# Row-to-column turning of the expert tiles: PE transposes against block-wise ScalarE writes and VectorE 32x32 turns

## The reference

```python
x = x + autocorrelation(layernorm(x), ctx, ctx)      # 8 heads, top 12 lags, soft-weighted shifted sums
n = layernorm(x)                                      # (x - mean) / sqrt(var + 1e-5), 2048 features
q = n @ Wq.T                                          # 16 values per row
scores = q @ keys.T                                   # 64 experts
gate = softmax over the 16 best scores, 0 elsewhere
z = (n @ A.T) as 64 experts x 8, times gate           # 512 values per row
x = x + (z @ B.T) * 2.0
```

## Time and profile before

| what | us |
|---|---|
| median of 3 runs | 2157.5 (2156.28 to 2159.11) |
| the profiled execution, whole | 2156.57 |
| its span, first to last instruction | 2154.8 |
| one step of the expert tiles | 25.33 |

### The profile page before, as it was taken

The page is one execution under the profiler, slowest core; times in us unless marked ns, Lnnn a source line. Parts: engine busy times, 40 slices in busy tenths (PEclk is TensorE's granted clock), DMA queues, the critical chain, the costliest instruction groups (busy, mean ns, idle before and its releaser), DMA issues.

```text
span 2154.8 us, 29239 instructions
## 1 busy us (share of the span) xinstructions
PE 2115.7 (98%) x8920; PEld 1328.0 (62%) x8920; DVE 1673.8 (78%) x4051; ACT 1337.5 (62%) x3051; POOL 1561.3 (72%) x965
## 2 busy tenths in 40 slices
PE   5999999999999999999999999999999999999999
PEld 2455455455455455454454454888888888888887
DVE  7999999999999999999999999644444444444443
ACT  4786786786786786786765646644444455445441
POOL 6999999999999999999999988633343433333420
PEclk9999999999999999999999999999999999999999
DMA  7232333333333332333221246544545444444431
GB/s 282 97 108 103 120 111 103 120 111 103 121 109 103 121 109 103 122 109 103 103 89 64 83 168 239 171 158 166 175 164 174 159 166 165 158 166 172 164 119 59
DMA packets 110705, 287.50 MB, mean 133 GB/s; under 512 B 7168, under 2 KB 7296, under 8 KB 109568
## 3 DMA queue, kind: packets, MB, share of 16 engines
q1 hardware_dynamic: 110592, 286.19, 38.3%
HBM read 219.06 MB, written 67.11 MB: 133 GB/s over the span
## 4 chain that ended last, share of the span: by engine, by line
PE 82%; DVE 7%; POOL 6%; ACT 2%; issue 2%; DMA 1%; SPq 0%; DVEq 0%; ACTq 0%; POOLq 0%
PE pair L755 11%; PE pair L749 8%; PE out L581 6%; PE out L582 6%; PE out L583 6%; PE z L583 5%; PE z L582 5%; PE z L581 5%; PE pair L644 5%; PE evac L631 4%; PE evac L655 4%; PE evac L656 4%; PE lag L698 4%; PE pair L745 4%; PE tp L600 2%; POOL r_f L1804 2%
## 5 line engine op out<-in xcount | busy, mean ns | idle before, releaser
L1838 POOL TENSOR_TENSOR rows<-rows,cin 128x1024 f32<-128x1024 f32 x48 | 117.0, 2437 | 325.7 <-DMA rows<-out_dram 273.6
L755 PE MATMUL pair<-r_f,back 128*128 128x512 f32 x768 | 342.7, 597 | 0.5 <-DVE prod L1035 0.5
L1804 POOL TENSOR_TENSOR r_f<-prod 128x1024 f32<-128x1024 f32 x128 | 303.0, 2378 | 9.3 <-DVE prod L1033 7.4
L755 PEld LDWEIGHTS pair<-r_f,back 128*128 128x128 f32 x768 | 143.0, 190 | 192.7 <-issue 146.5
L749 PE MATMUL pair<-w_sb,wts 128*128 128x512 f32 x512 | 225.1, 592 | 1.4 <-ACT w_sb L1625 0.9
L1480 ACT ACTIVATE xn<-tp 128x512 f32<-128x512 f32 x94 | 55.1, 586 | 231.0 <-PE tp L600 230.9
L581 PE MATMUL z<-a_hi,xt 128*128 128x512 f32 x496 | 195.9, 395 | 0.0
L581 PE MATMUL out<-b_hi,zt_hi 128*128 128x512 f32 x492 | 194.3, 395 | 0.0
L583 PE MATMUL z<-a_hi,xt 128*128 128x512 f32 x496 | 193.4, 390 | 0.0
L582 PE MATMUL z<-a_lo,xt 128*128 128x512 f32 x496 | 193.3, 390 | 0.0
L582 PE MATMUL out<-b_lo,zt_hi 128*128 128x512 f32 x492 | 191.6, 389 | 0.0
(11 more groups left out here) (234 smaller groups left out, 5576.8 us busy)
## 6 DMA issues: line engine op xcount, KB each, us to landing
out_dram<-att_sb SPq DMA_DIRECT2D x32, 1024.0 KB, 4.2
rows<-out_dram SPq DMA_DIRECT2D x64, 512.0 KB, 3.8
cin<-out_dram SPq DMA_DIRECT2D x63, 512.0 KB, 4.0
xin<-in_x_dram SPq DMA_DIRECT2D x63, 512.0 KB, 4.1
vf<-in_ctx_dram SPq DMA_DIRECT2D x31, 1024.0 KB, 5.1
out_dram<-rows SPq DMA_DIRECT2D x62, 512.0 KB, 2.8
xf<-in_x_dram SPq DMA_DIRECT2D x30, 1024.0 KB, 5.3
stat_in<-in_x_dram SPq DMA_DIRECT2D x27, 1024.0 KB, 5.1
```

Source lines behind the costliest of these rows:

```text
L755: return nc.tensor.matmul(pair_ps[:, bank, :], back[:, 3 * bank + n, :], r_f[:, row, :], start=n == 0, stop=n == 2)
L1804: nc.gpsimd.tensor_tensor(dst, prod[:, slot, 0:2, :], prod[:, slot, 2:4, :], ALU.add).then_inc(add_done, 1)
L1838: nc.gpsimd.tensor_tensor(half, first, other, op).then_inc(c_added, 1)
```

## The change

For tiles 4 to 31 (`spread(t)`) PE's 16 transposes and ACT's four copies out of PSUM go. In their place ACT writes the normalized rows in 16 operations of 32 partitions x 512 (`norm_blocks`): rows of partition group c and features of group b go to partition group b, column block c. DVE then turns `xn` in place in four operations of 128x512, each made of 32x32 blocks (`turn_spread`). Together these make the full transpose, with the features in another order, which the host gives to A and Wq as well (`laid_out`), and `norm_rows` to tiles 0 to 3. The low part is now taken from `xt_full` in SBUF, not from PSUM. Of the 16 blocks, 12 are written at the end of the ACT step before, behind `tile_scale` and `copy_queries`, the last four behind `zt_high`. PE makes the queries of tile u+1 ahead of the last output bank of step u. DVE's order changes: the first half of the statistics goes ahead of the turns, the turns ahead of route, the second half and tile_mean ahead of gate_z, and invert_root ahead of add_out 2.

```diff
@@ -247,6 +247,7 @@
         x2_added, stat2_step, root2_done, norm2_ready = (
             sem("x2_added"), sem("stat2_step"), sem("root2_done"), sem("norm2_ready"))
         xn_ready, tp_ready = sem("xn_ready"), sem("tp_ready")
+        xn_part = sem("xn_part")
         tp_hi, tp_lo, tp_full = sem("tp_hi"), sem("tp_lo"), sem("tp_full")
         q_ready, q_copied, sc_ready, sc_copied = sem("q_ready"), sem("q_copied"), sem("sc_ready"), sem("sc_copied")
         route_step, gate_exp, gate_step, gate_ready = (
@@ -384,8 +385,19 @@
 
             return xt[:, low, 0:KN, :] if is_step(u, TT) else (zt_lo if low else zt_hi)[:]
 
+        FIRST_SPREAD = 4
+        SPREAD = P // 4
+        SPREAD_PARTS = 16
+
+        def spread(t):
+            return not (isinstance(t, int) and t < FIRST_SPREAD)
+
         def later_tile(u):
             return not (isinstance(u, int) and u + 2 >= TT)
+
+        def ahead(u):
+
+            return later_tile(u) and spread(u + 2)
 
         def each_tile(eng, body):
             body(0, -1, 3, True, False, True)
@@ -833,8 +845,9 @@
                     queries(0, 2)
                     queries(0, 3)
                 elif a and not is_step(u, 1):
-                    for q in range(4):
-                        queries(u, q)
+                    if is_step(u, 2):
+                        for q in range(4):
+                            queries(u, q)
                     pe.wait_ge(tp_lo, tp_at(u, 3) + 1)
                 def turn_z(t=u):
                     pe.wait_ge(zg_ready, t)
@@ -891,14 +904,17 @@
                                         b_hi[:, q, m, :], b_lo[:, q, m, :], m == 0, m == KN - 1)
                     last.then_inc(out_ready, 1)
 
-                if f and not is_step(u, 0):
+                if f and not (is_step(u, 0) or spread(u + 1)):
                     for q in range(4):
                         turn_tile(u + 1, q)
                 if b:
-                    if not f:
+                    if not f or spread(u + 1):
                         pe.wait_ge(zt_hi_done, u)
                         pe.wait_ge(zt_lo_done, u)
                     for q in range(4):
+                        if q == 3 and f and not is_step(u, 1):
+                            for part in range(4):
+                                queries(u + 1, part)
                         out_bank(q)
                         if is_step(u, TT - 1) and q == 1:
                             turn_z(TT)
@@ -992,8 +1008,16 @@
 
                 dve.wait_ge(tp_hi, tp_at(t, q) + 1)
                 part = slice(4 * q, 4 * q + 4)
-                nc.vector.tensor_tensor(xt[:, 1, part, :], tp_ps[bank_of(t, q)][:], xt[:, 0, part, :].bitcast(F32),
+                turned_x = xt_full[:, q, :, :] if spread(t) else tp_ps[bank_of(t, q)][:]
+                nc.vector.tensor_tensor(xt[:, 1, part, :], turned_x, xt[:, 0, part, :].bitcast(F32),
                                         ALU.subtract).then_inc(tp_lo, 1)
+
+            def turn_spread(t, q):
+
+                if q == 0:
+                    dve.wait_ge(xn_part, SPREAD_PARTS * (t - FIRST_SPREAD + 1))
+                part = xn[:, q * 512:(q + 1) * 512]
+                nc.vector.transpose(part, part).then_inc(tp_full, 1)
 
             def half_statistics(t, slot, h):
                 dve.wait_ge(x2_added, 2 * t + h + 1)
@@ -1359,30 +1383,33 @@
                     return
                 if not is_step(u, TT):
                     zt_low()
+                if later_tile(u):
+                    half_statistics(u + 2, (r + 3) % RING, 0)
+                if f and spread(u + 1):
+                    for q in range(4):
+                        turn_spread(u + 1, q)
                 if a:
                     route()
                 if f:
                     tile_low(u + 1, 0)
+                add_out(0)
+                if f:
                     tile_low(u + 1, 1)
-                add_out(0)
-                if a:
-                    gate_z()
-                if f:
-                    tile_low(u + 1, 2)
-                if later_tile(u):
-                    half_statistics(u + 2, (r + 3) % RING, 0)
-                add_out(1)
-                if f:
-                    tile_low(u + 1, 3)
                 if later_tile(u):
                     half_statistics(u + 2, (r + 3) % RING, 1)
                     tile_mean(u + 2)
+                if a:
+                    gate_z()
+                add_out(1)
+                if f:
+                    tile_low(u + 1, 2)
+                    tile_low(u + 1, 3)
                 if is_step(u, TT - 1):
                     zt_low(TT)
+                if later_tile(u):
+                    invert_root(u + 2)
                 add_out(2)
                 add_out(3)
-                if later_tile(u):
-                    invert_root(u + 2)
 
             each_tile(dve, tile_step)
 
@@ -1476,8 +1503,9 @@
 
             def tile_high(t, q):
                 n = tp_at(t, q)
-                act.wait_ge(tp_ready, n + 1)
-                nc.scalar.activation(xt_full[:, q, :, :], tp_ps[bank_of(t, q)][:], ACT.Copy).then_inc(tp_full, 1)
+                if not spread(t):
+                    act.wait_ge(tp_ready, n + 1)
+                    nc.scalar.activation(xt_full[:, q, :, :], tp_ps[bank_of(t, q)][:], ACT.Copy).then_inc(tp_full, 1)
                 act.wait_ge(tp_full, n + 1)
                 nc.scalar.activation(xt[:, 0, 4 * q:4 * q + 4, :], xt_full[:, q, :, :], ACT.Copy).then_inc(tp_hi, 1)
 
@@ -1506,8 +1534,22 @@
 
             def norm_rows(t, slot):
                 act.wait_ge(norm2_ready, 2 * t + 2)
-                nc.scalar.activation(xn[:], rows[slot][:], ACT.Identity, bias=shift2[:],
-                                     scale=rstd2[:]).then_inc(xn_ready, 1)
+                nc.scalar.activation(xn[:].rearrange("p (k b i) -> p b k i", b=4, k=KD),
+                                     rows[slot][:].rearrange("p (b k i) -> p b k i", b=4, k=KD),
+                                     ACT.Identity, bias=shift2[:], scale=rstd2[:]).then_inc(xn_ready, 1)
+
+            def norm_blocks(t, slot, blocks):
+
+                if blocks[0] == 0:
+                    act.wait_ge(norm2_ready, 2 * t + 2)
+                    act.wait_ge(tp_lo, tp_at(t - 1, 3) + 1)
+                by_block = xn[:].rearrange("p (k c i) -> p k c i", k=KD, c=4)
+                for c in blocks:
+                    own = slice(SPREAD * c, SPREAD * (c + 1))
+                    for b in range(4):
+                        nc.scalar.activation(by_block[SPREAD * b:SPREAD * (b + 1), :, c, :],
+                                             rows[slot][own, b * 512:(b + 1) * 512].rearrange("p (k i) -> p k i", k=KD),
+                                             ACT.Identity, bias=shift2[own], scale=rstd2[own]).then_inc(xn_part, 1)
 
             act.wait_ge(consts_set, 2)
             nc.scalar.activation(inv_sum[:, 0:1], consts[:, 1:2], ACT.Sqrt)
@@ -1694,10 +1736,10 @@
             steps(body)
 
             def tile_step(u, k, r, a, b, f):
-                def copy_queries():
-                    act.wait_ge(q_ready, 4 * u + 4)
-                    if b:
-                        act.wait_ge(sc_ready, u)
+                def copy_queries(t=u):
+                    act.wait_ge(q_ready, 4 * t + 4)
+                    if not is_step(t, 0):
+                        act.wait_ge(sc_ready, t)
                     nc.scalar.activation(q_sb[:], sc_ps[:, 0:P], ACT.Copy).then_inc(q_copied, 1)
 
                 def zt_high():
@@ -1716,7 +1758,7 @@
                     act.wait_ge(route_step, 5 * u + 4)
                     nc.scalar.activation(best_exp[:], best[:], ACT.Exp, bias=best_neg[:], accum_out=gate_sum[:]).then_inc(gate_exp, 1)
 
-                if a:
+                if is_step(u, 0) or is_step(u, 1) or is_step(u, 2):
                     copy_queries()
                 if is_step(u, 0):
                     norm_tile(1, 1)
@@ -1745,9 +1787,11 @@
                     act.wait_ge(stored, 16 * GROUPS)
                     part_high(7)
                 else:
-                    if f:
-                        norm_tile(u + 1, (r + 2) % RING)
+                    if is_step(u, 2):
+                        norm_tile(3, 3)
                     zt_high()
+                    if f and spread(u + 1):
+                        norm_blocks(u + 1, (r + 2) % RING, (3,))
 
                 if f:
                     for q in range(4):
@@ -1760,6 +1804,12 @@
                     exponentials()
                 if later_tile(u):
                     tile_root(u + 2)
+                    if ahead(u):
+                        tile_scale(u + 2)
+                if f and not is_step(u, 1):
+                    copy_queries(u + 1)
+                if ahead(u):
+                    norm_blocks(u + 2, (r + 3) % RING, (0, 1, 2))
 
             each_tile(act, tile_step)
 
@@ -1957,12 +2007,12 @@
     if name in _INS[:2]:
         return a[:, ROWS, :]
     if name == "L0_ffn_A_w":
```

(4 more changed lines are left out.)

## The result

The changed kernel takes 2181.8 us (median, 2181.4 to 2183.2) beside 2158.2 us of the kernel before on the same chip: ratio 1.0112, 95% interval 1.0094 to 1.0129. It is slower by 23.5 us, past the upper end of the range (2173). The forecast was 2137.

What follows compares the result with a forecast made beforehand. PE's list alone set the old 25.33 us step; the new loop was ACT 13.53 + DVE 10.89 + lock 0.25 = 24.67 us, a gain of 20.9 from 2157.5, so 2137 us, range 2120 to 2173.

Steps and rivals of the forecast that it cites:

- ACT's side: ACT's part of the round, from invert_root through 16 blocks at 0.706 us each, with handovers: 13.53 us.
- DVE's shorter side: DVE's part of the round, from the four turns to invert_root: 10.89 us forecast.
- the lock: DVE's tile_low 0, now with both operands in SBUF, may wait for POOL's add: 0.52 us in full, 0.25 taken.
- Rival 1: ACT's blocks don't overlap when the partition group changes: 1.5 us more a round, slower, 2170 us; chance 0.28.
- P: Length of the ACT and DVE round on the expert tiles, forecast as 24.67 us.
- the loop: Blocks on ACT, then turns and statistics on DVE, back to the blocks; expected to set the new step instead of PE.
- The turn: DVE's four turns of 128x512, priced like a plain copy at 0.61 us each, 2.44 in all.
- Rival 2: DVE's turn costs double: 2.1 us more a round, P = 26.55, 2187 us; chance 0.05.
- Rival 4: Nothing of the loop binds, blocks near 0.54 us: all 46.8 us gained, 2111 us; chance 0.08.
- PE's floor: PE's step without the transposes, nothing else late: 25.33 - 1.67 = 23.66 us.
- The edits at nothing: Moved queries and reordered DVE work, held to cost nothing, with PE waiting about a microsecond before the last output bank.
- Head start and end: Tile 4's blocks begin 1.8 us before z of tile 3; the last two tiles go at PE's pace.

Runs made afterwards that it cites:

- the series of eight: Changed kernel plus series of eight ScalarE operations of 512 columns behind its last store: 0.706 us apart with start groups kept, 0.826 with either side's changing.
- the kernel that keeps its groups: Changed kernel with each of the 16 blocks written to the partition group it was read from (result not the reference's): 2150.6 us, ratio 0.9972.

## Why the prediction was wrong, and where it was right

**The step that failed** is the price of a block, in *ACT's side*: 0.706 taken from the earlier trace rows, with 0.80 as the upper bound. Measured in the kernel: (10.02 - 0.81) / 11 = 0.837. Both are wrong for one reason. In the earlier trace rows each operation starts at the partition where the last one did and begins 0.09 us before that one's end; here each starts in another group and begins 0.03 us after it. "No overlap at all" was therefore no ceiling: between end and start lies a gap of its own. Over the round, 1.57 us came on for the twelve blocks, 0.40 for the four and 0.13 for zt_high between them, 2.10 in all, which DVE's shorter side, tile_scale and the lock that did not occur cut to 1.57.

**Rival 1** has the right mechanism, shown by the series of eight and by the kernel that keeps its groups, and the right sign. Its time was 2170: it counted 0.094 for a block, where 0.13 came on, P = 25.92 against 26.25, and 27 rounds of 0.33 are 8.9 of the 12 us missing. Its break-even (P = 25.44, a block of 0.77) was not tried at that point; the loop of 25.0 came out faster, that of 26.25 slower. I gave it 0.28, because function and columns were the same. The feature that was not the same, the start partition, was named there and outweighed by the resemblance of the rest.

**The frame held.** The loop, and not a sum of busy time, sets the step; the turns start on the sixteenth block and ACT on the inverse root; the round's sum with measured terms is 26.24 for 26.25 us. 1.67 us a step left PE and none of it arrived.

**The turn** costs 0.61 us from start to start (2.49 for four), as taken from a copy. Rival 2 falls. The estimate of 0.71 from the figure of the Trainium skill, VectorE: DVE Perf Modes, section The three transpose paths, is not far from the 0.68 that one turn takes by itself.

**The lock** is there, and is gone at P = 26.25 as rival 1 had it: in the changed kernel POOL's adds end before tile_low 0. That one round of the kernel that keeps its groups shows 0.58 where 0.52 was forecast is partly luck: over its rounds the wait lies between nothing and 1.75 us, 0.4 on the mean. What I missed is what it does in shorter rounds.

**Rival 4**, with all 46.8 us gained once blocks are cheap, is false as it stood. Half the blocks gave 2136, not 2111: the loop through store, reload, POOL's adds and the first statistics half takes over, with 24.3 in the round shown. The prediction had the parts of that loop, 1.19 for the statistics half, 9.63 from the turns to the end of add_out 1 and 11.6 to the end of the two adds, but never summed them: 22.4 us, under PE's floor. What lifts them above it is tile_low's wait for POOL, which lies in this loop too and grew to 1.9 us. PE's floor itself was right: 23.75 measured for 23.66.

**The edits at nothing** cost 0.10 us a step, about 3 of the some 4 us in all. PE's one expected wait of about a microsecond before the last bank came as 1.71 before bank 2, which waits for add_out 0, and 0.42 before bank 3. I had followed only the bank whose add had been moved, and not the turns' delay of all of them.

**Head start and end** were mis-sized by 3.4 us together (1.4 and 2.1): the head start did not come, and PE's pace was not reached in the last step. Open stays why the queries between the output banks cost 0.10 us.

## What to carry to other kernels

When a price is taken from a row of the same function and size, compare the start partitions as well: cutting a wide operation into blocks on alternating partition groups costs a follow-up 0.83 us in place of 0.71 here, and sixteen of them turned a gain into a loss. Write down every loop that returns to the same buffer, with its length, before shortening one: the next one, here 24.3 us through the store and reload, is what a reordering runs into. Here two edits, one that shortens the first loop and one that lengthens the distance in the second, gave some 40 us together, where one alone gave 6 and the other lost 58.

## What the hardware showed that I had not expected

ScalarE starts a follow-up 0.09 us before the end of the last one when both begin in the same partition group (0.706 us apart), and 0.01 to 0.03 us after it when either side's start group changes (0.826 in the series, 0.837 in the tiles). It makes no difference whether it is the input, the output or both, and 32 partitions take as long as 128. The Trainium skill, ScalarE: Activation LUTs, section What ACT_TABLE_LOAD costs, gives an overlap of about 93 ns for back-to-back operations; the trace agrees only while the group stays. VectorE does the same, 0.46 against 0.55 us.

VectorE's turn of a 128x512 fp32 tile passes beside POOL's adds undisturbed (2.49 us for four), and so does a subtraction with one operand in PSUM, while scale-and-shift with two per-partition operands, one wide input only, waits for POOL as a subtraction of two SBUF tiles does (9.88 and 11.00 us for four).
